# A state-space scan kernel: a small product moved from GpSimd to ScalarE, ScalarE's work reordered, weight loads of the last block spread

## The chip, the cores and the metric

The kernel runs on one NeuronCore of one Trainium2 chip. The metric is the time of one execution on the device, in microseconds. The kernel before took 2678.2 us, the median of three runs (2674.68 to 2682.89).

## The reference, cut to what matters

The input x has the shape (2, 2048, 512). The first half of the model is a small linear recurrence (64 states) followed by a Mamba layer; the second half is a feed-forward layer with quantised activations and weights. What the change touches lies in the Mamba layer:

```python
xb = silu(conv(x_br) + conv_b)                      # 1024 channels
Bm, Cm = xb @ W_b, xb @ W_c                         # 16 states each
delta = softplus(xb @ W_delta + b_delta)
A_bar = exp(delta[..., None] * A)
Bx = delta[..., None] * Bm[:, :, None, :] * xb[..., None]
def step(h, inp):
    a_t, bx_t, c_t = inp
    h = a_t * h + bx_t
    return h, sum(h * c_t[:, None, :], axis=-1)
h0, ys = scan(step, ...)
y = ys + xb * Dp                                    # the product that is moved
out = y * silu(z) @ W_out                           # silu(z) is done at another place
```

The feed-forward half needs its two weights of 4 MB each (`f_w1`, `f_w2`) in SBUF when it starts, and 16 rows of a low-rank factor, made from sixteen 1 MB pieces of `c2_w2` (the chunks).

## The kernel before, in words

The two sequences of 2048 steps are cut into 16 blocks of 256 steps. Within a block the 1024 channels times 16 states are cut into 32 tiles q: channel tile dt = q // 4 (128 channels), state group g = q % 4 (4 states). One tile is a 128x1024 array. Four engines work on each tile:

- ScalarE makes the decay `a_ps` of the tile with four exponentials (L691). There are two such buffers: it may begin tile q when the scan of tile q-2 is over.
- VectorE makes the input term of tile q+1 in a ring of four slots (L845) and then scans tile q (L853).
- GpSimd keeps the last column (L462) and multiplies the scanned states by C in two halves (L469).
- TensorE transposes and sums the result into `yT_ps` (L1056). For each channel tile it first brings in x times D, `xdp` (L1050), which GpSimd makes at g == 0 (L456). VectorE then multiplies by silu(z) into `gbuf` (L788).

Every engine has its own written-out order, and it runs it in order. Between the tiles of block k stand the jobs that prepare block k+1 ("front", `next_plan`), finish the scan's own inputs ("scan", `scan_plan`) and finish block k-1 ("back", `back_plan`). A number in those tables is the tile q before whose exponentials the job stands on ScalarE; TensorE has its own table, with its own numbers. TensorE's jobs go through two PSUM banks, `work0` and `work1`, handed over by the counters `full` and `free`. The jobs of which the prediction speaks:

- DL0 to DL3 are the four parts of `xb @ W_delta` (L1022). TensorE's table has the last quarters of DL1 at 24, of DL2 at 29 and of DL3 at 31. ScalarE takes each with `dexp` (two Abs, L600, two Relu, L602), and each pair of them goes on through `dtail` (Exp, L609) and `dln` (Ln, L613); GpSimd adds the two halves (L420).
- PRJ is the projection of the small recurrence (last part: L932, at 2 in TensorE's table). ScalarE takes it with an Exp (L497) and a Tanh (L500), later an Ln (L505). VectorE's small recurrence, whose first instruction is L746, stands between its scans of tiles 4 and 5 and waits for this Ln.
- `zsilu` is silu(z) (L582). It needs another table of functions, and the exponentials after it need the old one back: an ACT_TABLE_LOAD ahead of it and one behind.

In the last block SyncE's queue carries the chunks and both feed-forward weights. TensorE multiplies the chunks (L1098, two columns) at fixed tiles, the second one at q = 11.

Of the kernel before, what the change touches and what calls it, by code (L numbers as in the profile page):

```python
# [5 lines left out]
ALU = mybir.AluOpType  # L6
ACT = mybir.ActivationFunctionType
# [68 lines left out]
def scan_phase(nc, V, big, s_big, vec, xT_in, w_p, w_s, w_o, w_in, w_bc, w_delta, w_out, f_w1, f_w2, c2_w1, c2_w2,  # L76
# [3 lines left out]
    with ctx:  # L80
# [175 lines left out]
        def _(sp):  # L256
# [11 lines left out]
            def step(k, par, front, back, scan):  # L268
# [19 lines left out]
                if last:

                    sp.wait_ge(full[BANK["WOUT1"]], jobs_before("WOUT1", k) + 1)  # L290
                    sp.dma_start(big[0][:, 0:7 * DI], f_w1[:, 0:7 * DI]).then_inc(s_big[0], 16)
                    sp.dma_start(big[1][:, :], f_w2).then_inc(s_big[1], 16)

                    def keep_row(c):
                        sp.wait_ge(s_rowcp, c + 1)
                        sp.dma_start(lr_dram[c], xw[:, c % 2, :]).then_inc(s_rowst[c % 2], 16)

                    for c in range(1, NCH):
                        if c == 1:
                            sp.wait_ge(full[BANK["WOUT1"]], jobs_before("WOUT1", k) + 1)  # L300
                        if c == 2:
                            sp.wait_ge(s_h, 1)
                        if c >= 3:
                            sp.wait_ge(s_row, c - 2)
                            keep_row(c - 3)
                        sp.dma_start(chunk[(c + 1) % 3], c2_w2[c]).then_inc(s_chunk[c % 3], 16)
                    sp.wait_ge(s_col0, NCOL * NBLK)
                    sp.dma_start(big[0][:, 7 * DI:8 * DI], f_w1[:, 7 * DI:8 * DI]).then_inc(s_big[0], 16)
                    for c in range(NCH - 3, NCH):
                        keep_row(c)  # L310
                    for i in range(2):
                        sp.wait_ge(s_rowst[i], 16 * NCH // 2)
# [39 lines left out]
        def _(pool):  # L352
# [69 lines left out]
            def step(k, par, front, back, scan):  # L422
                for q in range(NQ):
# [25 lines left out]
                            r.then_inc(s_cpow, 1)  # L449
                    if not scan:  # L450
                        continue
                    if g == 0:

                        wait(pool, s_xb, 2 * k + (2 if dt >= ND // 2 else 1))
                        wait(pool, s_tr, NQ * k + NG * (dt - 2) + 1)
                        nc.gpsimd.tensor_tensor(xdp[:, dt % 2, :], xb[:, par, dt, :],  # L456
                                                V[:, V_DP + dt:V_DP + dt + 1].to_broadcast([P, T]), ALU.mult)\
                            .then_inc(s_xdp, 1)

                    pool.wait_ge(s_scan, NQ * k + q + 1)  # L460
                    h = ring[:, q % RING, :, :]
                    nc.gpsimd.tensor_tensor(carry[:, par, dt, G * g:G * g + G].rearrange("p (g o) -> p g o", o=1),  # L462
# [12 lines left out]
        def _(act):  # L475
# [9 lines left out]
            def step(k, par, front, back, scan):  # L485
# [6 lines left out]
                def prj():  # L492

                    ps = take("PRJ")
                    if isinstance(k, int) and k == -1:
                        act.wait_ge(s_setD, 8)
                    nc.scalar.activation(e0[:, :], ps[0:N0, 0:T], ACT.Exp, bias=sc0[0:N0, 4:5]).then_inc(s_e0, 1)  # L497

                    wait(act, s_c0, 6 * n)
                    nc.scalar.activation(c0[:, :], ps[N0:P, 0:T], ACT.Tanh, bias=sc0[N0:P, 4:5]).then_inc(s_tanh, 1)  # L500

                def prj_ln():
                    nc.scalar.preload_act_table_set("natural_log_exp_and_others")
                    act.wait_ge(s_c0, 6 * n + 1)
                    nc.scalar.activation(e0[:, :], e0[:, :], ACT.Ln, bias=1.0).then_inc(s_l0, 1)  # L505

# [69 lines left out]
                def zsilu():  # L576

                    for j in (2, 3):
                        act.wait_ge(free[BANK[f"Z{j}"]], jobs_before(f"Z{j}", k) + 1)
                    for tt in range(NT):  # L580
                        v = zs[:, fp, tt, :]
                        r = nc.scalar.activation(v, v, ACT.Silu)  # L582
                    r.then_inc(s_zs, 1)

# [35 lines left out]
                def gT(pair, gp):  # L620
# [3 lines left out]
                                         ps[:, :].rearrange("p (m t) -> p m t", m=2), ACT.Copy)\  # L624
                        .then_inc(free[BANK[f"GT{pair}"]], 1)

                def gelu():
                    act.wait_ge(s_h, 1)
                    for m in range(KD):
                        r = nc.scalar.activation(hT[:, m, :], work[0][:, 8 + 2 * m:8 + 2 * m + 2], ACT.Gelu,  # L630
                                                 bias=V[:, V_C2B1 + m:V_C2B1 + m + 1])
                    r.then_inc(s_hT, 1)

                def rowcopy(c):
# [4 lines left out]
                    else:  # L639
# [1 line left out]
                    nc.scalar.activation(xw[:, c % 2, :], work[0][0:2, :], ACT.Copy).then_inc(s_rowcp, 1)  # L641


                next_plan = {5: [prj], 6: [prj_ln], 8: [lambda: stats(0)], 9: [lambda: stats(1)], 10: [y0scale],
                             11: [y0back], 14: [lambda: xcopy(0)], 15: [lambda: xcopy(1)], 16: [lambda: xcopy(2)],
                             17: [lambda: xcopy(3), silu], 20: [bc], 21: [lambda: zcopy(0)], 23: [lambda: zcopy(1)],
                             25: [lambda: dexp(0, False)], 27: [lambda: zcopy(2), lambda: dexp(1, False), lambda: dtail(0, False)],
                             28: [lambda: zcopy(3), lambda: dln(0, False)], 30: [zsilu],
                             31: [lambda: dexp(2, False)]}
                scan_plan = {2: [lambda: dexp(3, True), lambda: dtail(1, True)], 6: [lambda: dln(1, True)]}  # L650
                turned = {13: 0, 20: 1, 28: 2}
                back_plan = {6: [lambda: gT(ND // 2 - 1, fp)], 9: [lambda: wout(0)], 12: [lambda: wout(1)]}
                for q in range(NQ + 1):
# [496 lines left out]
def ffn_phase(nc, V, big, s_big, x_in, x2_dram, lr_dram, c2_b2, base, b1, b2, out):  # L1150

    ctx = ExitStack()
    with ctx:
# [21 lines left out]
        with setup:  # L1175
# [39 lines left out]
            def _(act):  # L1215

                for i, q in enumerate((q1, q2)):
                    act.wait_ge(s_big[i], 32 if i == 0 else 16)
                    nc.scalar.activation(q[:, :, :].rearrange("p a b -> p (a b)"), big[i][:, :], ACT.Abs,
                                         accum_out=mq[:, i:i + 1]).then_inc(z["abs"], 1)  # L1220

# [439 lines left out]
```

## Time and profile before

| | |
|---|---|
| median of three runs | 2678.2 us (2674.68 to 2682.89) |
| profiled execution, its own time | 2683.99 us |
| span of the profiled execution | 2681.9 us |
| mean granted clock of TensorE | 0.948 |
| busy, share of the span | TensorE 86%, weight loads 59%, VectorE 84%, ScalarE 62%, GpSimd 64% |
| first and last scan (L853) start | 118.9 and 2157.2 us |

Busy times of different engines lie beside each other and don't add up. The part from the first scan to the last is three quarters of the span. In the lists of waits a row names the instruction that waited, then what released it. The chain of waits that the page prints lies for the most part in the feed-forward half, so it says little about the blocks; there the timeline has to be read.

### The profile page before, as it was taken

The numbers are of one execution on the slowest core, as the hardware profiler recorded it, in microseconds if no ns is written. First come the engines' busy times: TensorE is split into PE (matmuls) and PEld (weight loads), VectorE is DVE, ScalarE is ACT, GpSimd is POOL, SyncE is SP. The second block draws the span as 40 slices with busy tenths as digits, with TensorE's granted clock in tenths as the row PEclk, the third lists the DMA queues.
The fourth block names the chain that finished last, engine by engine and source line by source line (L and its number), as shares of the span: only waits on it lengthen the run. The fifth ranks groups of instructions, "written<-read, shape, count | busy, mean of one in ns | idle before, by whom it ended". The sixth has DMA issues, their size and how long they took to land. (4 is left out here: it accounts for less than half of the span.)

```text
span 2681.9 us, 34173 instructions
## 1 busy us (share of the span) xinstructions
PE 2307.7 (86%) x11488; PEld 1590.2 (59%) x11520; DVE 2265.7 (84%) x2232; ACT 1665.4 (62%) x3332; POOL 1725.8 (64%) x2042
## 2 busy tenths in 40 slices
PE   7878888889898988888988888898986884999997
PEld 5656666666666665766666666666664332444443
DVE  2299999999999999999999999999997735888886
ACT  2566676666667676667676767667674434555554
POOL 0287777878787877878787878787876521232221
PEclk8889999999999999999999999999997987999999
DMA  4102020202011110202020202010114421112110
GB/s 184 72 1 71 9 74 7 75 11 74 17 63 45 36 64 17 72 10 71 9 71 9 75 5 79 17 63 25 48 57 178 175 100 55 60 59 66 63 52 24
DMA packets 47435, 151.74 MB, mean 57 GB/s; under 512 B 7973, under 2 KB 8869, under 8 KB 44206
## 3 DMA queue, kind: packets, MB, share of 16 engines
q1 hardware_dynamic: 47278, 149.76, 15.8%
q8 instruction: 84, 1.38, 0.2%
q14 instruction: 73, 0.60, 0.1%
HBM read 132.37 MB, written 17.37 MB: 56 GB/s over the span
## 5 line engine op out<-in xcount | busy, mean ns | idle before, releaser
L469 POOL TENSOR_TENSOR ring<-ring,Cbc 128x512 f32<-128x512 f32 x1024 | 1281.8, 1273 | 44.6 <-POOL carry L462 0.4
L853 DVE TENSOR_TENSOR_SCAN ring<-a_ps,ring 128x1024 f32<-128x1024 f32 x512 | 1168.0, 2282 | 99.3 <-ACT a_ps L691 97.9
L691 ACT ACTIVATE a_ps<-delta,nA 128x255 f32<-128x255 f32 x2048 | 850.0, 466 | 382.2 <-DVE ring L853 381.0
L1056 PE MATMUL yT_ps<-ident,ring 128*128 128x128 f32 x4096 | 586.0, 284 | 171.2 <-POOL ring L469 168.7
L845 DVE TENSOR_TENSOR ring<-u_ps,Bbc 128x1024 f32<-128x1024 f32 x512 | 619.7, 1210 | 38.1 <-PE yT_ps L1056 31.3
L1056 PEld LDWEIGHTS yT_ps<-ident,ring 128*128 128x128 f32 x4096 | 474.1, 144 | 287.9 <-POOL ring L469 245.6
L1022 PE MATMUL work<-xb,big 128*128 128x256 f32 x2048 | 474.5, 383 | 11.1 <-ACT zs L557 11.1
L1022 PEld LDWEIGHTS work<-xb,big 128*128 128x128 f32 x2048 | 384.4, 192 | 80.1 <-issue 17.8
L462 POOL TENSOR_TENSOR carry<-ring,half 128x4 f32<-128x4 f32 x512 | 126.0, 246 | 380.4 <-DVE ring L853 378.8
L1038 PE MATMUL work<-Wout,xb 128*128 128x512 f32 x512 | 242.1, 608 | 0.0
L995 PE MATMUL work<-y0s,big 128*128 128x256 f32 x1024 | 235.1, 380 | 0.7 <-issue 0.7
L1396 POOL TENSOR_TENSOR m<-m,pows 128x1 f32<-128x1 f32 x64 | 34.1, 548 | 311.0 <-DVE m L1528 311.0
L995 PEld LDWEIGHTS work<-y0s,big 128*128 128x128 f32 x1024 | 188.8, 190 | 24.7 <-issue 1.0
L1038 PEld LDWEIGHTS work<-Wout,xb 128*128 128x128 f32 x512 | 100.4, 201 | 120.4 <-issue 120.4
L1463 PE MATMUL o_ps<-q,qhT 128*128 128x512 bf16 x481 | 112.1, 386 | 18.9 <-DVE qhT L1561 18.7
L420 POOL TENSOR_TENSOR delta<-delta,lnbuf 128x1024 f32<-128x1024 f32 x32 | 75.5, 2361 | 74.4 <-ACT lnbuf L613 74.4
L1427 PE MATMUL x_ps<-lay,x2T 128*128 128x512 f32 x256 | 121.9, 621 | 0.7 <-ACT x2T L1488 0.7
L564 ACT ACTIVATE xb<-work,V 128x256 f32<-128x256 f32 x128 | 53.3, 467 | 103.9 <-PE work L995 103.9
L1442 PE MATMUL h_ps<-q,qaT 128*128 128x512 bf16 x511 | 115.5, 379 | 0.1
L1494 ACT ACTIVATE hb<-hb 128x2048 f32<-128x2048 f32 x32 | 61.1, 1911 | 65.8 <-DVE hb L1547 65.8
L824 DVE TENSOR_TENSOR u_ps<-delta,xb 128x510 f32<-128x510 f32 x64 | 58.5, 914 | 48.0 <-POOL delta L420 48.0
L1011 PE MATMUL work<-xb,Wbc 128*32 128x256 f32 x256 | 70.2, 437 | 33.2 <-ACT xb L573 33.2
(198 smaller groups left out, 2538.9 us busy)
## 6 DMA issues: line engine op xcount, KB each, us to landing
Bbc<-bc_rows SPq DMA_DIRECT2D x64, 512.0 KB, 4.6
Cbc<-bc_rows SPq DMA_DIRECT2D x64, 512.0 KB, 3.7
xT<-in_xT SPq DMA_DIRECT2D x16, 514.0 KB, 3.6
x_rows<-x2row SPq DMA_DIRECT2D x32, 256.0 KB, 2.0
xp<-x_rows SPq DMA_DIRECT2D x32, 256.0 KB, 2.7
xx<-in_x SPq DMA_DIRECT2D x32, 256.0 KB, 3.0
out_rows<-orow SPq DMA_DIRECT2D x32, 256.0 KB, 2.0
delta<-in_c_w SPq DMA_DIRECT2D x6, 1024.0 KB, 5.1
```

The lines of the kernel that those rows point to most:

```text
L462: nc.gpsimd.tensor_tensor(carry[:, par, dt, G * g:G * g + G].rearrange("p (g o) -> p g o", o=1), h[:, :, T - 1:T], ident1, ALU.mult).then_ ...
L469: nc.gpsimd.tensor_tensor(hp, hp, Cbc[:, G * g + GP * c:G * g + GP * c + GP, :], ALU.mult)\
L691: r = nc.scalar.activation(a_ps[q % 2][:, i, 1:T], delta[:, par, dt, 1:T], ACT.Exp, scale=nA[:, dt, s:s + 1])
L845: dve.tensor_tensor(ring[:, q % RING, :, :], u_ps[:, dt % 2:dt % 2 + 1, :].to_broadcast([P, G, T]), Bbc[:, G * g:G * g + G, :], ALU.mult). ...
L853: dve.tensor_tensor_scan(ring[:, q % RING, :, :].rearrange("p g t -> p (g t)"), a_ps[q % 2][:, :, :].rearrange("p g t -> p (g t)"), ring[: ...
L995: r = pe.matmul(ps[:, T * m:T * m + T], Mx[:, tap, c:c + P], y0s[:, fp, tap:tap + T], start=(tap == 0), stop=(tap == 3))
L1022: r = pe.matmul(ps[:, T * m:T * m + T], Wd[:, d, c:c + P], xb[:, fp, d, :], start=(d == 0), stop=(d == ND - 1))
L1038: r = pe.matmul(ps[:, :], xb[:, fp, d, P * tt:P * tt + P], Wout[:, d, :], start=False, stop=(d == ND - 1))
L1056: r = pe.matmul(yT_ps[:, tt, :], ring[:, q % RING, i, P * tt:P * tt + P], ident[:, :], is_transpose=True, start=False, stop=(g == NG - 1 a ...
L1427: r = pe.matmul(x3_ps[:, :], x2T[:, d, :], lay[:, batch, d, :], start=(d == 0), stop=(d == KD - 1))
L1442: r = pe.matmul(h_ps[:, 512 * c:512 * c + 512], qaT[:, d, :], q1[:, d, 512 * c:512 * c + 512], start=(d == 0), stop=(d == KD - 1))
L1463: r = pe.matmul(o_ps[:, :], qhT[:, d, :], q2[:, d, :], start=(d == 0), stop=(d == KF - 1))
```

## The change

Three parts:

1. `xdp` is made by ScalarE (`skip`, an ACT.Copy with D as its scale), at the last tile of the channel tile before: at q = 3, 7, ... 27 for dt+1, and at q = 29 for the first channel tile of the next block. GpSimd has none of it left.
2. ScalarE's jobs stand at other tiles. The Exp of PRJ goes from 5 to 3. silu(z) goes from 30 of the block before to 4 of the block that uses it, the Tanh goes with it to 4, one table load ahead of both and one behind. `dexp(0)` goes from 25 to 24, `dexp(1)` from 27 to 26, `dln(0)` from 28 to 27, `dexp(3)` from 2 to 1. The table load ahead of the Ln at 6 is gone.
3. In the last block `f_w2` is loaded early, behind the first chunk, and `f_w1` in eight pieces, one behind each of the chunks 2 to 8 and the last as before. Before, both were issued ahead of chunk 1.

```diff
                     sp.dma_start(chunk[1], c2_w2[0]).then_inc(s_chunk[0], 16)
+                    sp.wait_ge(full[BANK["DL3"]], jobs_before("DL3", k - 1) + 1)
+                    sp.dma_start(big[1][:, :], f_w2).then_inc(s_big[1], 16)
...
-                    sp.wait_ge(full[BANK["WOUT1"]], jobs_before("WOUT1", k) + 1)
-                    sp.dma_start(big[0][:, 0:7 * DI], f_w1[:, 0:7 * DI]).then_inc(s_big[0], 16)
-                    sp.dma_start(big[1][:, :], f_w2).then_inc(s_big[1], 16)
...
                         sp.dma_start(chunk[(c + 1) % 3], c2_w2[c]).then_inc(s_chunk[c % 3], 16)
+                        if 2 <= c < 9:
+                            sp.dma_start(big[0][:, DI * (c - 2):DI * (c - 1)], f_w1[:, DI * (c - 2):DI * (c - 1)])\
+                                .then_inc(s_big[0], 16)
...
-                    if g == 0:
-                        wait(pool, s_xb, 2 * k + (2 if dt >= ND // 2 else 1))
-                        wait(pool, s_tr, NQ * k + NG * (dt - 2) + 1)
-                        nc.gpsimd.tensor_tensor(xdp[:, dt % 2, :], xb[:, par, dt, :],
-                                                V[:, V_DP + dt:V_DP + dt + 1].to_broadcast([P, T]), ALU.mult)\
-                            .then_inc(s_xdp, 1)
...
+                def skip(b, bp, dt):
+                    wait(act, s_xb, 2 * b + (2 if dt >= ND // 2 else 1))
+                    wait(act, s_tr, NQ * b + NG * (dt - 2) + 1)
+                    nc.scalar.activation(xdp[:, dt % 2, :], xb[:, bp, dt, :], ACT.Copy, scale=V[:, V_DP + dt:V_DP + dt + 1])\
+                        .then_inc(s_xdp, 1)
...
+                    if q == 4 and (front or scan):
+                        nc.scalar.preload_act_table_set("silu_and_others")
+                        if scan:
+                            zsilu()
+                        if front:
+                            prj_tanh()
+                        nc.scalar.preload_act_table_set("natural_log_exp_and_others")
...
+                    if scan and g == 3 and dt < ND - 1:
+                        skip(k, par, dt + 1)
+                    if front and q == NQ - 3:
+                        skip(n, fp, 0)
```

ScalarE, first tiles of a block, the kernel before, from the exponentials of tile 2 (the L691 row ahead of L497 holds tiles 2, 3 and 4):

```order
L600 ACTIVATE lnbuf<-work,V 128x256
L602 ACTIVATE delta<-work,V 128x256
L609 ACTIVATE lnbuf<-lnbuf 128x1024
L691 ACTIVATE a_ps<-delta,nA 128x255 x12
L497 ACTIVATE e<-work,sc 64x256
L500 ACTIVATE c<-work,sc 64x256
L691 ACTIVATE a_ps<-delta,nA 128x255 x4
L623 ACTIVATE xb<-work 128x512
L503 ACT_TABLE_LOAD
L505 ACTIVATE e<-e 64x256
L613 ACTIVATE lnbuf<-lnbuf 128x1024
L691 ACTIVATE a_ps<-delta,nA 128x255 x8
```

The same place in the changed kernel, from tile 1 on (L707 are the exponentials, L628 is `xdp`, L492 and L498 the Exp and Tanh of PRJ, L579 is silu(z)):

```order
L707 ACTIVATE a_ps<-delta,nA 128x255 x4
L606 ACTIVATE lnbuf<-lnbuf 128x1024
L707 ACTIVATE a_ps<-delta,nA 128x255 x4
L492 ACTIVATE e<-work,sc 64x256
L628 ACTIVATE xdp<-xb,V 128x256
L707 ACTIVATE a_ps<-delta,nA 128x255 x4
L674 ACT_TABLE_LOAD
L579 ACTIVATE zs<-zs 128x1024 x2
L498 ACTIVATE c<-work,sc 64x256
L679 ACT_TABLE_LOAD
L707 ACTIVATE a_ps<-delta,nA 128x255 x8
L620 ACTIVATE xb<-work 128x512
```

The Exp of PRJ and `xdp` now stand ahead of the exponentials of tile 3, and two table loads with silu(z) and the Tanh between them ahead of those of tile 4.

ScalarE, tiles 25 to 29 of a block, before (L557 copies z):

```order
L691 ACTIVATE a_ps<-delta,nA 128x255 x8
L557 ACTIVATE zs<-work 128x512
L600 ACTIVATE lnbuf<-work,V 128x256
L602 ACTIVATE delta<-work,V 128x256
L600 ACTIVATE lnbuf<-work,V 128x256
L602 ACTIVATE delta<-work,V 128x256
L609 ACTIVATE lnbuf<-lnbuf 128x1024
L691 ACTIVATE a_ps<-delta,nA 128x255 x4
L557 ACTIVATE zs<-work 128x512
L613 ACTIVATE lnbuf<-lnbuf 128x1024
L623 ACTIVATE xb<-work 128x512
L691 ACTIVATE a_ps<-delta,nA 128x255 x8
```

And now, from tile 24 on (L597 and L599 are `dexp`, L554 copies z, L606 and L610 are `dtail` and `dln`):

```order
L707 ACTIVATE a_ps<-delta,nA 128x255 x8
L597 ACTIVATE lnbuf<-work,V 128x256
L599 ACTIVATE delta<-work,V 128x256
L597 ACTIVATE lnbuf<-work,V 128x256
L599 ACTIVATE delta<-work,V 128x256
L707 ACTIVATE a_ps<-delta,nA 128x255 x4
L554 ACTIVATE zs<-work 128x512
L606 ACTIVATE lnbuf<-lnbuf 128x1024
L610 ACTIVATE lnbuf<-lnbuf 128x1024
L628 ACTIVATE xdp<-xb,V 128x256
L707 ACTIVATE a_ps<-delta,nA 128x255 x4
L554 ACTIVATE zs<-work 128x512
```

`dexp(1)` now stands ahead of the exponentials of tile 26; before, it stood ahead of those of tile 27, behind the copy of z.

SyncE's queue in the last block, before (L279 and L281 are the first two loads for the factor rows, L286 stores results, L291 and L292 are the two weights, L306 the chunks, L296 stores a row of the factor):

```order
L279 DMA delta<-in_c_w 128x2048
L281 DMA zs<-in_c_w 128x2048
L286 DMA x_rows<-x2row 128x512 x2
L291 DMA big<-in_f_w 128x7168
L292 DMA big<-in_f_w 128x8192
L306 DMA xb<-in_c_w 128x2048
L306 DMA delta<-in_c_w 128x2048
```

And now:

```order
L281 DMA zs<-in_c_w 128x2048
L284 DMA big<-in_f_w 128x8192
L289 DMA x_rows<-x2row 128x512 x2
L305 DMA xb<-in_c_w 128x2048
L305 DMA delta<-in_c_w 128x2048
L308 DMA big<-in_f_w 128x1024
L295 DMA lr_rows<-lnbuf 2x512
```

`f_w2` stands ahead of the stores of results, and chunk 1 directly behind them.

## Rows read from the trace of the kernel before

**Rows 1.** Waits of the whole span: who, released by, us in total, times, longest

```profile
DVE ring L853 <- ACT a_ps L691: 97.9, 62, 4.0
DVE ring L845 <- PE yT_ps L1056: 31.3, 17, 22.6
```

**Rows 2.** Timeline, VectorE, tiles 23, 26, 27, 31 (start, duration, [idle before])

```profile
964.87 2.28 DVE L853 TENSOR_TENSOR_SCAN ring<-a_ps,ring 128x1024 f32<-128x1024 f32 x1
...
975.13 2.28 DVE L853 TENSOR_TENSOR_SCAN ring<-a_ps,ring 128x1024 f32<-128x1024 f32 x1
...
979.66 2.29 DVE L853 TENSOR_TENSOR_SCAN ring<-a_ps,ring 128x1024 f32<-128x1024 f32 x1 [0.91 <-ACT a_ps L691]
...
994.22 2.29 DVE L853 TENSOR_TENSOR_SCAN ring<-a_ps,ring 128x1024 f32<-128x1024 f32 x1 [0.89 <-ACT a_ps L691]
```

**Rows 3.** Timeline, TensorE, the same stretch: transpose of tile 23, DL1, DL2

```profile
970.07 0.66 PE L1056 MATMUL yT_ps<-ident,ring 128*128 128x128 f32 x4 [0.56 <-POOL ring L469]
970.56 3.62 PE L1022 MATMUL work<-xb,big 128*128 128x256 f32 x16
...
985.35 7.07 PE L1022 MATMUL work<-xb,big 128*128 128x256 f32 x32
```

**Rows 4.** Timeline, ScalarE, the same stretch

```profile
975.07 0.60 ACT L557 ACTIVATE zs<-work 128x512 f32<-128x512 f32 x1 [2.91 <-PE work L1003]
...
976.99 1.08 ACT L609 ACTIVATE lnbuf<-lnbuf 128x1024 f32<-128x1024 f32 x1
977.94 1.69 ACT L691 ACTIVATE a_ps<-delta,nA 128x255 f32<-128x255 f32 x4
...
984.73 1.28 ACT L582 ACT_TABLE_LOAD   x1
986.02 2.00 ACT L582 ACTIVATE zs<-zs 128x1024 f32<-128x1024 f32 x2
```

**Rows 5.** Timeline, start of the next block, several engines: DL3, PRJ, tiles 0, 4 and L746

```profile
999.61 0.47 ACT L600 ACTIVATE lnbuf<-work,V 128x256 f32<-128x256 f32 x1 [1.40 <-PE work L1022]
...
1000.89 2.28 DVE L853 TENSOR_TENSOR_SCAN ring<-a_ps,ring 128x1024 f32<-128x1024 f32 x1
...
1001.05 1.07 ACT L609 ACTIVATE lnbuf<-lnbuf 128x1024 f32<-128x1024 f32 x1
...
1006.73 1.95 PE L932 MATMUL work<-xT,Ws 128*64 128x256 f32 x8
...
1015.27 2.27 DVE L853 TENSOR_TENSOR_SCAN ring<-a_ps,ring 128x1024 f32<-128x1024 f32 x1
...
1018.12 0.47 DVE L746 SCALAR_TENSOR_TENSOR e<-work,sc,e 64x256 f32<-64x256 f32 x1 [0.58 <-ACT e L505]
```

**Rows 6.** Groups by line of the whole span: count, busy us, mean ns

```profile
L456 POOL TENSOR_TENSOR xdp<-xb,V 128x256 f32<-128x256 f32 x128 | 78.9, 617 | 0.1
...
L602 ACT ACTIVATE delta<-work,V 128x256 f32<-128x256 f32 x128 | 60.4, 472 | 0.0
```

**Rows 7.** Timeline, last block, TensorE: chunks 1 and 2

```profile
2079.59 6.07 PE L1098 MATMUL work<-xb,Wtap 128*2 128x512 f32 x8 [18.45 <-DMA xb<-in_c_w]
...
2087.49 3.59 PE L1098 MATMUL work<-delta,Wtap 128*2 128x512 f32 x8
```

**Rows 8.** Timeline, last block, SyncE's DMA issues

```profile
2056.11 0.43 SPq L291 DMA_DIRECT2D big<-in_f_w  x1
...
2057.08 0.43 SPq L306 DMA_DIRECT2D xb<-in_c_w  x1
```

**Rows 9.** The page's DMA issues: KB each, median us from issue to landing

```profile
delta<-in_c_w SPq DMA_DIRECT2D x6, 1024.0 KB, 5.1
```

**Rows 10.** Timeline, VectorE and GpSimd at two changes of block

```profile
745.20 0.67 DVE L824 TENSOR_TENSOR u_ps<-delta,xb 128x510 f32<-128x510 f32 x1
...
995.13 2.50 POOL L469 TENSOR_TENSOR ring<-ring,Cbc 128x512 f32<-128x512 f32 x2
996.42 1.77 DVE L824 TENSOR_TENSOR u_ps<-delta,xb 128x510 f32<-128x510 f32 x1
```

More of the change, by code:

```diff
@@ L497, in prj, with prj_tanh @@
                     nc.scalar.activation(e0[:, :], ps[0:N0, 0:T], ACT.Exp, bias=sc0[0:N0, 4:5]).then_inc(s_e0, 1)
+                def prj_tanh():
+                    ps = take("PRJ")
                     wait(act, s_c0, 6 * n)
@@ L502, in prj_ln @@
                 def prj_ln():
-                    nc.scalar.preload_act_table_set("natural_log_exp_and_others")
                     act.wait_ge(s_c0, 6 * n + 1)
@@ L578, in zsilu @@
                     for j in (2, 3):
-                        act.wait_ge(free[BANK[f"Z{j}"]], jobs_before(f"Z{j}", k) + 1)
+                        act.wait_ge(free[BANK[f"Z{j}"]], jobs_before(f"Z{j}", k - 1) + 1)
                     for tt in range(NT):
-                        v = zs[:, fp, tt, :]
+                        v = zs[:, par, tt, :]
                         r = nc.scalar.activation(v, v, ACT.Silu)
@@ L641, in rowcopy @@
                     nc.scalar.activation(xw[:, c % 2, :], work[0][0:2, :], ACT.Copy).then_inc(s_rowcp, 1)
-                next_plan = {5: [prj], 6: [prj_ln], 8: [lambda: stats(0)], 9: [lambda: stats(1)], 10: [y0scale],
+                next_plan = {3: [prj], 6: [prj_ln], 8: [lambda: stats(0)], 9: [lambda: stats(1)], 10: [y0scale],
                              11: [y0back], 14: [lambda: xcopy(0)], 15: [lambda: xcopy(1)], 16: [lambda: xcopy(2)],
                              17: [lambda: xcopy(3), silu], 20: [bc], 21: [lambda: zcopy(0)], 23: [lambda: zcopy(1)],
[L647 to L650, printed above, removed]
+                             24: [lambda: dexp(0, False)], 26: [lambda: dexp(1, False)],
+                             27: [lambda: zcopy(2), lambda: dtail(0, False), lambda: dln(0, False)],
+                             28: [lambda: zcopy(3)], 31: [lambda: dexp(2, False)]}
+                scan_plan = {1: [lambda: dexp(3, True)], 2: [lambda: dtail(1, True)], 6: [lambda: dln(1, True)]}
                 turned = {13: 0, 20: 1, 28: 2}
@@ L1217, in _ @@
                 for i, q in enumerate((q1, q2)):
-                    act.wait_ge(s_big[i], 32 if i == 0 else 16)
+                    act.wait_ge(s_big[i], 16 * (F * KD // DI) if i == 0 else 16)
                     nc.scalar.activation(q[:, :, :].rearrange("p a b -> p (a b)"), big[i][:, :], ACT.Abs,
```

## The prediction, made before the changed kernel was run

> **What bounds the kernel now.** I read three views, in this order.
>
> The list of waits first. VectorE is busy 84% of the span, and in the blocks it is the engine that the others wait for. What holds VectorE itself up is the first row: its scans wait 97.9 us for ScalarE's exponentials, in 62 places, and its input terms wait 31.3 us for TensorE, of which 22.6 us is one single wait [rows 1].
>
> Then VectorE's timeline of one block, to see at which tiles those waits lie. The 97.9 us are some 6 us in each of 16 blocks; 0.91 us stands ahead of tile 27 and 0.89 ahead of tile 31 [rows 2], and the largest one stands behind the first silu of a block (tile 17), whose place the change leaves alone. Since nothing else stops the scans of a block, each us by which ScalarE comes late for a tile is a us of the block, and each us freed on an engine that waits is nothing.
>
> Then ScalarE and TensorE beside it, for the question that decides here: at the place where a job stands now, is its input there, and how much room is there before the scan?
>
> **GpSimd's product.** GpSimd loses 128 products of 617 ns, 78.9 us in all [rows 6]. It is no gain by itself: GpSimd waits for VectorE's scans. ScalarE gets the 128. The trace has no Copy of this shape from SBUF; the nearest row is a Relu of 128x256 with a mean of 472 ns [rows 6], and four instructions of that kind go from 999.61 to 1001.05, 0.36 us a piece, because each overlaps the one before [rows 5]. I take 0.36 (0.3 to 0.47). At most tiles ScalarE idles before its exponentials and covers it; where it is already late, at tiles 3 and 27, the 0.36 is in the sums below. Its buffer and its inputs are ready several tiles ahead.
>
> **The end of a block (tiles 26 to 31).** `dexp(1)` moves one tile forward, but its input does not. TensorE first transposes tile 23, for which it waits for GpSimd and so for the scan of tile 23 (start 964.87), and then runs the 16 instructions of DL1's last half, from 970.56 for 3.62 us: DL1 is full at 974.18, 9.31 us after the start of scan 23 [rows 2, 3]. Before, ScalarE took it behind the copy of z at 975.07, where it had waited 2.91 us with the exponentials of tile 26 already done [rows 4]. Now these exponentials stand behind it. 974.18 + 0.04 + 1.44 (`dexp`) + 1.67 (four exponentials) + 0.03 = 977.36, where scan 26 started at 975.13 [rows 2, 4, 5]: 2.2 us late. None of the 9.31 us is work that the change takes away.
>
> Tile 27: the exponentials of 26 leave the engine's entrance at 977.26; the copy of z takes 0.50, `dtail` 0.95 (976.99 to 977.94), `dln` as much and 0.13 for waiting on its end, `xdp` 0.36: 980.14, and the exponentials end at 981.85 where scan 27 stood at 979.66 [rows 2, 4]. Still 2.2 late; the 0.91 that was idle is used up in it.
>
> Tiles 28 to 30 have room, and at 30 silu(z) is gone: table load 1.28, 2.00 for two functions, and one load more [rows 4]. But tile 31 stands behind `dexp(2)`, which needs DL2. TensorE began this stretch at 985.35, 5.69 after scan 27, and DL2 is full after 24 of the 32 instructions, 5.3 us on [rows 2, 3]. With scan 27 at 981.86 this gives 992.85, and + 0.04 + 1.44 + 1.67 + 0.03 = 996.03, where scan 31 started at 994.22. So the block ends **1.8 us later**. The gain of moving silu(z) away is at most the waits at 30 and 31, and most of it is lost again in DL2. Bounds: below, the 0.9 us that the waits of 27 and 31 could give back if DL1 came early (-2.6 with tile 30); above, 2.2.
>
> **The start of a block (tiles 1 to 5).** `dexp(3)` at 1: it started at 999.61, waiting for TensorE [rows 5]. Behind it now come the exponentials of tile 1, done by 1002.8, while scan 0 (1000.89 to 1003.17) still runs: covered.
>
> The Exp of PRJ at 3: PRJ is full at 1006.73 + 1.95 = 1008.68, 7.79 after scan 0 [rows 5]. The exponentials of tile 3 now stand behind this Exp. One after the other from 1008.72: Exp 0.45, `xdp` 0.36, exponentials of tile 3 1.67, load 1.28, two silu 2.00, Tanh 0.43, load 1.28, exponentials of tile 4 1.67, and 0.03 to the scan: 1017.9, where scan 4 started at 1015.27 [rows 4, 5, 6]: 2.6 us late. Part of it comes back at once. VectorE's small recurrence (L746) waited 0.58 us for the Ln behind a table load that is gone. Now ScalarE does the exponentials of tile 5 (1.6), the copy of GT3 (0.6) and the Ln (0.42) from 1017.8: 1020.4, against 1018.12 [rows 5]. The start costs **2.3 us**. Bounds: 0 if PRJ came 2.3 us earlier, 2.4 with the dearer `xdp`.
>
> [...]
>
> **Sum over blocks.** Fifteen blocks of 16 have a next one to prepare: 15 x (1.8 + 2.3) = 61.5 us. In the first block there is no work of a block before, and DL3 is late there; I leave 3 us either way. In the last block neither the Exp nor the Tanh is there, and silu with two loads (4.56) fits ahead of tile 4; silu(z) in the run-up before block 0 stood in a wait for TensorE.
>
> **The last block.** The 22.6 us wait is this: the feed-forward weights were issued at 2056.11, chunk 1 behind them at 2057.08 [rows 8], and TensorE waited 18.45 us for it; the product then took 6.07 instead of the 3.59 of the next one [rows 7]. Now chunk 1 goes out about 2056.1, a lone chunk lands in 5.1 us [rows 9], so at 2061.2, and TensorE is there at 2079.59 - 18.45 = 2061.14. The pieces of 512 KB go behind chunks that are waited for only later, and `f_w2` runs when nothing else is under way. Gain 18.45 + 2.48 = **20.9 us** (15, if the pieces delay a chunk; 22.6 at most, the whole wait).
>
> **Total.** 2683.99 (the profiled execution's own time) + 61.5 - 20.9 = 2724.6 us. That execution lay 5.8 over the median of the runs, so for the median: 2678.2 + 40.6 = **2719 us**. The case's own range is 2706 to 2731: 15 blocks by +-0.6 us, the last block and the first by some us.
>
> **Rivals.**
>
> *The reordering is covered* (faster). Place: tiles 26 and 4. It decides from the point at which DL1 and PRJ are full 2.2 us and 2.6 us earlier against the scans. For it: GpSimd, which TensorE waits for, has less to do. Against it: TensorE waits at 970.07 for tile 23's product with C, and GpSimd makes that as soon as the scan is over, with `xdp` elsewhere [rows 3]. Then the block waits fall by 2.6 in 15 blocks and the last block gives 20.9: 2678.2 - 39 - 20.9 = 2618; with only the stalls gone, 2657. Chance 0.07.
>
> *Only one of the two delays is there* (no change, or little). If PRJ were early and tile 26 late: 2678.2 + 15 x 1.8 - 20.9 = 2684; the other way round 2692. Nothing in the rows speaks for it. Chance 0.06, half of it within the bound.
>
> *VectorE gets past GpSimd at the change of block* (slower, but less). L824 took 1.77 us at 996.42, while a GpSimd instruction ran, and 0.67 us at 745.20 [rows 10]. GpSimd's place in time at the end of a block shifts with the change, by less than one of its 1.25 us instructions by my reckoning. If VectorE comes first in 14 blocks: 2719 - 15.4 = 2704. [...] Chance 0.12.
>
> *The last block's wait moves instead of going* (slower still). If a chunk behind the pieces is late by what is now gone: 2678.2 + 61.5 = 2740. Against it: seven pieces of 512 KB over seven rows of the factor, each behind its chunk in the queue, and a lone chunk needs 5.1 us. Chance 0.07.
>
> **How the numbers follow.** Forecast 0.68, rivals 0.07, 0.06, 0.12, 0.07. The range of 8 in 10 is 2692 to 2733: it takes in the forecast's own range and the rival with the lock, and leaves the faster one and most of the last out. A change within 0.3% (8 us) is what a measurement of this kernel can't tell from none. Faster by more: 0.07. Within: 0.04. Slower by more: 0.89.
>
> **What would show it.** Right: scans of tile 26 wait some 2.2 us and of tile 4 some 2.6 us for ScalarE's exponentials, in 15 blocks; the time from one block's first scan to the next grows by about 4; VectorE's total wait for exponentials rises from 97.9 to over 150 us; the row of 22.6 is gone and TensorE's wait for chunk 1 is under 1 us. Wrong: the Abs of DL1 starts without idle time ahead of it at tile 26, or the second chunk still waits.

## The result, and the profile after

The changed kernel takes 2726.7 us (median of 4 runs, 2726.1 to 2737.9), the kernel before 2678.0 in the same series (2674.7 to 2682.9). The ratio is 1.019, with a 95% interval of 1.016 to 1.0221: some 49 us slower. The forecast was 2719 us, in a range of 2692 to 2733. The execution that was profiled is the longest of the four (2737.85 us, span 2736.1); the spans of the other three lie at 2723 to 2725.

The list of waits first (who, released by: us in total, times, longest), of the kernel after:

```profile
DVE ring L869 <- ACT a_ps L707: 175.6, 77, 6.4
...
DVE ring L861 <- PE yT_ps L1072: 17.8, 22, 2.9
```

L869 is the scan and L861 the input term. The scans wait for the exponentials 175.6 us instead of 97.9, and the wait of 22.6 us for the last block's weights is gone, the longest of its kind being 2.9 now [rows 1]. One grew by 78 us, the other shrank by 13.5.

VectorE's timeline of one block with its change to the next, for comparison with [rows 2, 5]; the rows are the scans of tiles 23, 26, 27 and 31, the first term of the next block (L840), its scans 0 and 4, and the small recurrence (L762):

```profile
997.99 2.28 DVE L869 TENSOR_TENSOR_SCAN ring<-a_ps,ring 128x1024 f32<-128x1024 f32 x1
...
1010.49 2.29 DVE L869 TENSOR_TENSOR_SCAN ring<-a_ps,ring 128x1024 f32<-128x1024 f32 x1 [2.15 <-ACT a_ps L707]
...
1015.00 2.29 DVE L869 TENSOR_TENSOR_SCAN ring<-a_ps,ring 128x1024 f32<-128x1024 f32 x1 [0.89 <-ACT a_ps L707]
...
1029.33 2.29 DVE L869 TENSOR_TENSOR_SCAN ring<-a_ps,ring 128x1024 f32<-128x1024 f32 x1 [1.77 <-ACT a_ps L707]
1031.54 1.42 DVE L840 TENSOR_TENSOR u_ps<-delta,xb 128x510 f32<-128x510 f32 x1
...
1035.65 2.28 DVE L869 TENSOR_TENSOR_SCAN ring<-a_ps,ring 128x1024 f32<-128x1024 f32 x1
...
1052.76 2.29 DVE L869 TENSOR_TENSOR_SCAN ring<-a_ps,ring 128x1024 f32<-128x1024 f32 x1 [2.64 <-ACT a_ps L707]
1055.28 0.47 DVE L762 SCALAR_TENSOR_TENSOR e<-work,sc,e 64x256 f32<-64x256 f32 x1 [0.23 <-ACT e L502]
...
1165.89 2.28 DVE L869 TENSOR_TENSOR_SCAN ring<-a_ps,ring 128x1024 f32<-128x1024 f32 x1
...
1297.26 2.28 DVE L869 TENSOR_TENSOR_SCAN ring<-a_ps,ring 128x1024 f32<-128x1024 f32 x1
```

From scan 23 to scan 26 it is 12.50 us here and was 10.26, to scan 27 17.01 and was 14.79, to scan 31 31.34 and was 29.35. From scan 0 to scan 4 it is 17.11 and was 14.38. This block goes from scan 0 at 1035.65 to the next one's at 1165.89, 130.24 us. Before, the fifteen blocks ahead of the last took 126.1 on average, and 126.15 in the steady ones. The next block here takes 131.37, more than the forecast has; that comes below.

ScalarE in the same stretch: `dexp(1)`, the exponentials of tile 26, and in the next block the Exp of PRJ, the silu group and the exponentials of tiles 4 and 5:

```profile
1007.33 0.47 ACT L597 ACTIVATE lnbuf<-work,V 128x256 f32<-128x256 f32 x1 [5.36 <-PE work L1038]
...
1008.78 1.68 ACT L707 ACTIVATE a_ps<-delta,nA 128x255 f32<-128x255 f32 x4
...
1043.49 0.47 ACT L492 ACTIVATE e<-work,sc 64x256 f32<-64x256 f32 x1 [2.78 <-PE work L948]
1043.86 0.50 ACT L628 ACTIVATE xdp<-xb,V 128x256 f32<-128x256 f32 x1
1044.26 1.66 ACT L707 ACTIVATE a_ps<-delta,nA 128x255 f32<-128x255 f32 x4
1045.94 1.28 ACT L674 ACT_TABLE_LOAD   x1
1047.23 2.01 ACT L579 ACTIVATE zs<-zs 128x1024 f32<-128x1024 f32 x2
...
1049.76 1.28 ACT L679 ACT_TABLE_LOAD   x1
1051.05 3.27 ACT L707 ACTIVATE a_ps<-delta,nA 128x255 f32<-128x255 f32 x8
```

ScalarE stands idle 5.36 us ahead of `dexp(1)`, with tile 26's exponentials behind it in the program and their input ready. Ahead of the Exp of PRJ it stands idle 2.78 us, with tile 3's behind it. And TensorE's side of both, DL1's last half, DL2 and PRJ:

```profile
1003.67 3.62 PE L1038 MATMUL work<-xb,big 128*128 128x256 f32 x16
...
1020.79 7.07 PE L1038 MATMUL work<-xb,big 128*128 128x256 f32 x32
...
1041.51 1.94 PE L948 MATMUL work<-xT,Ws 128*64 128x256 f32 x8
```

DL1 is full at 1003.67 + 3.62 = 1007.29, 9.30 us after scan 23 (9.31 before). PRJ is full 7.80 us after scan 0 (7.79 before), and DL2 starts 5.79 us after scan 27 (5.69 before). TensorE keeps its distance to the scans, so a job of ScalarE that is put one tile forward still starts only when TensorE is through, and what stands behind the job waits with it.

In the last block, TensorE's product of chunk 1:

```profile
2134.60 3.59 PE L1114 MATMUL work<-xb,Wtap 128*2 128x512 f32 x8 [1.25 <-ACT lnbuf L645]
```

It waits 1.25 us, here for ScalarE and no longer for the DMA, where it had waited 18.45, and takes 3.59 instead of 6.07 us [rows 7]. From scan 12 to scan 13 of the last block it is 6.63 us and was 26.31.

### The profile page after: what moved, and what is told of

Same layout as the page of the kernel before. It is cut to its first block and busy times, and to the rows that moved or that the text cites. A ratio compares the mean times of both kernels' runs of the same rounds, so it can differ in the third digit from the quotient of the medians.

```text
span 2736.1 us, 34209 instructions
## 1 busy us (share of the span) xinstructions
PE 2338.7 (85%) x11520; PEld 1608.2 (59%) x11520; DVE 2261.6 (83%) x2232; ACT 1692.6 (62%) x3443; POOL 1657.4 (61%) x1914
## 5 line engine op out<-in xcount | busy, mean ns | idle before, releaser
L869 DVE TENSOR_TENSOR_SCAN ring<-a_ps,ring 128x1024 f32<-128x1024 f32 x512 | 1168.3, 2282 | 175.6 <-ACT a_ps L707 175.6
L707 ACT ACTIVATE a_ps<-delta,nA 128x255 f32<-128x255 f32 x2048 | 852.0, 468 | 221.5 <-DVE ring L869 220.6
L1072 PEld LDWEIGHTS yT_ps<-ident,ring 128*128 128x128 f32 x4096 | 482.5, 146 | 272.8 <-POOL ring L464 229.7
L861 DVE TENSOR_TENSOR ring<-u_ps,Bbc 128x1024 f32<-128x1024 f32 x512 | 620.1, 1211 | 24.5 <-PE yT_ps L1072 17.8
L1038 PE MATMUL work<-xb,big 128*128 128x256 f32 x2048 | 482.7, 388 | 39.1 <-ACT zs L554 39.1
L1054 PE MATMUL work<-Wout,xb 128*128 128x512 f32 x512 | 252.3, 629 | 0.0
L597 ACT ACTIVATE lnbuf<-work,V 128x256 f32<-128x256 f32 x128 | 60.9, 476 | 235.4 <-PE work L1038 235.4
L1054 PEld LDWEIGHTS work<-Wout,xb 128*128 128x128 f32 x512 | 102.9, 206 | 125.3 <-issue 125.3
L1479 PE MATMUL o_ps<-q,qhT 128*128 128x512 bf16 x512 | 119.2, 387 | 11.4 <-DVE qhT L1577 11.4
```

The source lines that it names most:

```text
L707: r = nc.scalar.activation(a_ps[q % 2][:, i, 1:T], delta[:, par, dt, 1:T], ACT.Exp, scale=nA[:, dt, s:s + 1])
L861: dve.tensor_tensor(ring[:, q % RING, :, :], u_ps[:, dt % 2:dt % 2 + 1, :].to_broadcast([P, G, T]), Bbc[:, G * g:G * g + G, :], ALU.mult). ...
L869: dve.tensor_tensor_scan(ring[:, q % RING, :, :].rearrange("p g t -> p (g t)"), a_ps[q % 2][:, :, :].rearrange("p g t -> p (g t)"), ring[: ...
L1038: r = pe.matmul(ps[:, T * m:T * m + T], Wd[:, d, c:c + P], xb[:, fp, d, :], start=(d == 0), stop=(d == ND - 1))
L1054: r = pe.matmul(ps[:, :], xb[:, fp, d, P * tt:P * tt + P], Wout[:, d, :], start=False, stop=(d == ND - 1))
L1072: r = pe.matmul(yT_ps[:, tt, :], ring[:, q % RING, i, P * tt:P * tt + P], ident[:, :], is_transpose=True, start=False, stop=(g == NG - 1 a ...
```

## The experiments

All times are medians; the interval is that of the ratio to the kernel before, in runs beside it.

**Only the loads spread** (the kernel before, with the last block's weight loads as in the kernel after):

```
+ sp.wait_ge(full[BANK["DL3"]], ...)                   # behind DL3 of the block before:
+ sp.dma_start(big[1][:, :], f_w2)
...
+ if 2 <= c < 9:                                      # behind chunk c
+     sp.dma_start(big[0][:, DI*(c-2):DI*(c-1)], f_w1[:, DI*(c-2):DI*(c-1)])
- sp.dma_start(big[0][:, 0:7*DI], f_w1[:, 0:7*DI])      # ahead of chunk 1
- sp.dma_start(big[1][:, :], f_w2)
```

> The kernel before with only the loads of the last block spread; all else as before. Theory (the wait for chunk 1 is a queue effect and goes): 2678 - 20.9 = 2657 us, VectorE's 22.6 us wait falls to about 2, the step from scan 12 to 13 of the last block from 26.3 to under 7. Rival (the wait moves to a later chunk): 2678, and a wait of TensorE for a DMA of over 10 us at another chunk.

Measured: 2660.5 us (2653.5 to 2665.6), ratio 0.9933 (0.9914 to 0.9953). The last block takes 124.4 us instead of 149.35, the others 126.1 on average as before. The product of the second chunk, for which TensorE had waited 18.45 us, now waits 1.24 us for it:

```profile
2053.48 3.59 PE L1101 MATMUL work<-xb,Wtap 128*2 128x512 f32 x8 [1.24 <-DMA xb<-in_c_w]
```

So this part is a gain by itself, and its mechanism is the forecast's: 18.45 - 1.24 of waiting and 2.48 of duration are 19.7 us, and from scan 12 to scan 13 it is 6.63 instead of 26.31 us, 19.7 as well. The medians differ by 18 us. The last block of the two traces differs by 25, of which the other 5.3 us are waits of VectorE for TensorE at tiles 9, 11 and 19 that are missing or shorter in this execution. The granted clock in the last block was 0.68 from 2040 to 2050 in the kernel before and 1.00 from 2025 on in this one, and the kernel after, with the same loads, has these waits again; so the 5.3 us belong to the execution and not to the loads. The profiled execution is also the fastest of its four, and its first scan starts at 113.7 us instead of 118.9, though nothing ahead of it was changed.

**Only the product on ScalarE** (the kernel before, with `skip` in place of GpSimd's product):

```
- nc.gpsimd.tensor_tensor(xdp[:, dt % 2, :], xb[:, par, dt, :], V[:, V_DP+dt:...], ALU.mult)
+ nc.scalar.activation(xdp[:, dt % 2, :], xb[:, bp, dt, :], ACT.Copy, scale=V[:, V_DP+dt:...])
```

> The kernel before with only the product of x and D moved to ScalarE. Theory (GpSimd's relief is worth nothing, ScalarE covers the product): 2676 to 2684 us, tile 27 later by 0.36 us, at the change of block L824 still blocked. Rival (GpSimd's relief lets VectorE past it and brings TensorE forward): 2660 or less, L824 at 0.67 us. Second rival (ScalarE is full and pays for each product): 2678 + 128 x 0.36 = 2724.

Measured: 2683.95 us, ratio 1.0014 (1.0004 to 1.0025). The row of the product by line (count, busy us, mean ns of one):

```profile
L623 ACT ACTIVATE xdp<-xb,V 128x256 f32<-128x256 f32 x128 | 64.5, 504 | 0.0
```

By its list of waits the scans wait 111.2 us for the exponentials, 13.3 us more than before, but the whole is only 5.5 us longer by the medians (1 to 7 by the interval). The product's duration is 504 ns, while two that follow each other start some 0.4 us apart: in the kernel after the Copy starts at 1043.86 and the exponentials at 1044.26.

The whole grows so little because two effects run against each other. By the starts of the scans, the steps up to tiles 27 and 30, where ScalarE is late, are 0.4 us longer each, 11.9 us in fifteen blocks; the step up to tile 9, where VectorE waits for TensorE, takes 3.6 us more in all (whether the product or a longer fall of TensorE's clock makes the latter isn't shown). Against that the change of block is 0.9 us shorter, 13.5 us in all, since VectorE's first term of a block now hardly meets GpSimd:

```profile
996.96 1.27 POOL L461 TENSOR_TENSOR ring<-ring,Cbc 128x512 f32<-128x512 f32 x1
...
997.98 0.80 DVE L827 TENSOR_TENSOR u_ps<-delta,xb 128x510 f32<-128x510 f32 x1
```

It takes 0.77 to 0.86 us at the fifteen changes of block, where it took 1.77 at fourteen of them [rows 10]. GpSimd's instruction starts 1.02 us ahead of it, and started 0.06 us ahead before. So the time fell just inside the expected range by a cancellation that the expectation did not have: it said that this term would still be blocked. The relief of GpSimd is worth 13.5 us at the change of block, by the rival's mechanism, and what the product costs elsewhere is slightly more.

**DL1's jobs back** (the kernel after, with the jobs of DL1 where they stood in the kernel before):

```
- 26: [dexp(1)], 27: [zcopy(2), dtail(0), dln(0)], 28: [zcopy(3)]
+ 27: [zcopy(2), dexp(1), dtail(0)], 28: [zcopy(3), dln(0)]
```

> The changed kernel with the two Abs, two Relu and Exp of DL1 back behind the copy of z at tile 27 and the Ln at 28. Theory (tile 26 waits for DL1 because of where dexp(1) stands): no wait at 26, 0.9 to 1.3 us at 27, the block 1.8 us shorter than in the changed kernel, about 2727 - 27 = 2700 us. Rival (the end of the block is late because ScalarE has the extra products): 2720 or more, the waits at 26 to 31 keep their sum.

Measured: 2707.2 us (2704.5 to 2710.8), ratio 1.0105 (1.0085 to 1.0125): 19.6 us less than the kernel after. Its scans of tiles 26, 27 and 31:

```profile
994.30 2.28 DVE L869 TENSOR_TENSOR_SCAN ring<-a_ps,ring 128x1024 f32<-128x1024 f32 x1
999.23 2.29 DVE L869 TENSOR_TENSOR_SCAN ring<-a_ps,ring 128x1024 f32<-128x1024 f32 x1 [1.32 <-ACT a_ps L707]
...
1013.46 2.29 DVE L869 TENSOR_TENSOR_SCAN ring<-a_ps,ring 128x1024 f32<-128x1024 f32 x1 [1.49 <-ACT a_ps L707]
```

The wait at 26 is gone, so `dexp(1)` at 26 made it. The kernel ends 7 us above the expectation: most of its blocks take 129.5 to 129.7, not 128.4, since at tiles 8 and 9 VectorE waits 1.4 to 1.7 us for TensorE (0.35 in the steady blocks before), the place at which some blocks of the kernel after are long, too.

**The silu group a tile later** (the kernel after, with the Exp of PRJ at 4 and the group at 5, ahead of tile 5's exponentials):

```
- next_plan = {3: [prj], 6: [prj_ln], ...        back_plan = {6: [gT(3)], ...
+ next_plan = {4: [prj], ...                     back_plan = {5: [gT(3)], ...
- if q == 4 and (front or scan):   # load, silu(z), tanh, load
+ if q == 5 and (front or scan):   # the same, and prj_ln() behind it
```

> The changed kernel with the two table loads, silu(z) and Tanh ahead of the exponentials of tile 5 instead of 4, the Exp of PRJ at 4 instead of 3, the copy of GT3 and the Ln of PRJ at 5. Theory (tile 5 has VectorE's small recurrence ahead of its scan, so 5 us of ScalarE fit there): no wait at tile 4, L746 about where it was before, the block 2.3 to 2.6 us shorter, and TensorE's clock does not fall at the start of blocks, together 2680 to 2692 us. Rival (silu(z) with two loads costs the same at any tile, as ScalarE has 5 us more at a stretch than its two buffers hold): 2720 or more, the wait moves to tile 5.

Measured: 2693.0 us (2692.1 to 2694.2), ratio 1.0048 (1.0031 to 1.0065): 33.7 us less than the kernel after, and 1 us above the expected range. Scans 0 and 4 and the small recurrence:

```profile
1141.15 2.28 DVE L871 TENSOR_TENSOR_SCAN ring<-a_ps,ring 128x1024 f32<-128x1024 f32 x1
...
1155.53 2.27 DVE L871 TENSOR_TENSOR_SCAN ring<-a_ps,ring 128x1024 f32<-128x1024 f32 x1
1158.62 0.48 DVE L764 SCALAR_TENSOR_TENSOR e<-work,sc,e 64x256 f32<-64x256 f32 x1 [0.82 <-ACT e L502]
```

From scan 0 to 4 it is 14.38 us again, as before, and the steady blocks take 128.1 (two of them 128.4). Tiles 26 and 31 still wait as in the kernel after, so the two delays are separate. No block is stretched at tiles 8 and 9: in the two traces fifteen blocks are 38.5 us shorter in all, more than 15 x 2.1. That TensorE's clock would not fall at the start of a block did not come true: it falls there in every block still (0.57 from 255 to 260, 0.75 in the next 5 us), for a shorter time.

**The jobs of DL1 and DL2 late** (the last kernel, with more of ScalarE's jobs moved):

```
- 26: [dexp(1)], 27: [zcopy(2), dtail(0), dln(0)], 28: [zcopy(3)], 31: [dexp(2)]
+ 27: [zcopy(2), dexp(1)], 28: [zcopy(3), dtail(0)], 29: [dln(0)], 32: [dexp(2)]
- scan_plan = {1: [dexp(3)], 2: [dtail(1)], 6: [dln(1)]}
+ scan_plan = {2: [dexp(3), dtail(1)], 6: [dln(1)]}
```

> The kernel after, with four groups of ScalarE's jobs put elsewhere: the silus and the tanh ahead of tile 5's exponentials (as in the run before), the two exponentials of delta that stood at tiles 26 and 30 moved to tile 27 and behind tile 31's last exponentials, the fourth one to tile 2 of the next block. Theory (each row of exps that comes late adds its time to VectorE's end): the waits of VectorE at tiles 26, 27 and 31, 4.7 us a block in the run before, go, the block takes 123.4 to 123.6 us instead of 128.1, and the kernel about 2621 us, faster than the kernel before as well. Rival (the exponential behind tile 31 delays the next block's first scans or TensorE's projection): a new wait of 1 to 3 us at tiles 0 to 2 takes the place, and the kernel stays above 2655 us.

Measured: 2632.0 us (2631.4 to 2635.2), ratio 0.9826 (0.9806 to 0.9846). The scans' wait for ScalarE is 61.3 us in all; at 26 and 31 there is none, and at 27 some 0.4 in most blocks. The kernel lies 11 us above the expectation, since the steady blocks take 124.3 to 124.7 us, not 123.5: a wait of 1.26 us is new ahead of the input term of tile 1, where the rival put one. Its mechanism is another, though. TensorE there, and VectorE's row that waits:

```profile
847.09 7.07 PE L1041 MATMUL work<-xb,big 128*128 128x256 f32 x32
854.00 0.38 PE L1069 MATMUL yT_ps<-ident,xdp 128*128 128x128 f32 x2
854.22 1.04 PE L1075 MATMUL yT_ps<-ident,ring 128*128 128x128 f32 x8
855.10 3.62 PE L1041 MATMUL work<-xb,big 128*128 128x256 f32 x16
858.55 1.04 PE L1075 MATMUL yT_ps<-ident,ring 128*128 128x128 f32 x8
```

```profile
859.62 0.16 DVE L855 TENSOR_REDUCE Bbc<-big 128x4 f32<-128x4 f32 x1 [1.26 <-PE yT_ps L1075]
```

TensorE has no idle time from 847.09 to the transposes at 858.55: it doesn't wait for the late exponentials, but is simply full, with 48 instructions of DL2 and DL3 ahead of what VectorE wants. With ScalarE's waits gone, TensorE is next. Whether another order of these products would help was not tried.

**The silu of x in two halves** (the last kernel, tile 17):

```
- 17: [xcopy(3), silu]           # load, silu of both halves, load
+ 17: [silu(0), xcopy(3), silu(1)]
```

> The kernel v1 with the silu at tile 17 cut into two halves: the first stands where ScalarE waits for the PSUM bank of the last copy of x (1.9 us), the second behind that copy, so that less work stands between tile 17's exponentials and the scan that wants them. Theory: VectorE's wait at tile 17, 3.6 us a block in all kernels so far, falls to about 1.7 us, the block by 2.0 us, the kernel by some 30 us against v1 (about 2591 us if v1 takes 2621). Rival (the wait at tile 17 is set by TensorE and not by ScalarE): no change against v1.

Measured: 2603.3 us (2602.3 to 2604.1), ratio 0.9714 (0.9695 to 0.9733). ScalarE at tile 17:

```profile
906.09 1.28 ACT L567 ACT_TABLE_LOAD   x1
907.38 1.06 ACT L572 ACTIVATE xb<-xb 128x1024 f32<-128x1024 f32 x1
908.35 0.82 ACT L561 ACTIVATE xb<-work,V 128x256 f32<-128x256 f32 x2
909.26 1.06 ACT L572 ACTIVATE xb<-xb 128x1024 f32<-128x1024 f32 x1
910.34 1.28 ACT L574 ACT_TABLE_LOAD   x1
```

The load and the first half fill the time in which ScalarE had waited 1.93 us for the product of the last x. VectorE's wait at tile 17 falls from 3.7 to 1.8 us, the block to 122.45. So at least half of the largest wait of a block, there in all kernels, was ScalarE's order and not TensorE.

**The product back on GpSimd** (the last kernel, with the multiplication where it stood in the kernel before).

> The kernel v2 with the product of x and D on GpSimd again, where it stood in the kernel before; ScalarE's order and the spread weight loads stay. Theory (the product's engine matters only where ScalarE is late, 0.36 to 0.4 us in one or two places of a block): within 8 us of v2, and rather below it. Rival (the relief of GpSimd is worth something once ScalarE's order is mended): more than 8 us slower than v2.

Measured: 2597.8 us (2594.0 to 2598.6), ratio 0.9691 (0.967 to 0.9711): 5.4 us less than the kernel with it on ScalarE. The size is that of the product's move alone, but the account differs: nearly all of it (6.0 us in fifteen blocks) stands in the step up to tile 27, and at the change of block VectorE's first term is short in both (0.67 us with the product on ScalarE, mostly 0.82 here). This is the fastest version, 3.1% below the kernel before. The spread loads, the later silu(z) with one table load less, and `dexp(0)` at 24 stem from the change; its other moves do not.

## Why the prediction was right

**The end of a block.** Forecast: scans of tiles 26, 27 and 31 later by 2.2, 2.2 and 1.8 us. Measured in the block above: 2.24, 2.22 and 1.99. `dexp(1)` starts 9.34 us after scan 23, 0.04 after DL1 is full, as the forecast has it. The experiment that puts these jobs back removes the wait at 26.

**The start of a block.** Forecast: scan 4 later by 2.6 us, of which 0.35 comes back at the small recurrence, 2.3 in all. Measured: 17.11 against 14.38, 2.73, with a wait of 0.23 instead of 0.58 at the recurrence, so 2.4. Moving the group by one tile gives back 2.1 us in each steady block (130.2 to 128.1), and the two ends are independent, as assumed: the waits at 26 and 31 stay.

**Their sum.** 4.1 us a block in the forecast, and 126.15 to 130.24 in five of the fourteen blocks behind the first. But four take 130.5 to 130.6 and five 131.3 to 131.8, so that with the first block fifteen came to 71.3 us more in the profiled execution, not 61.5. **This is the term that was too small.** In the fourteen blocks the excess over 4.1 us each is 7.7 us in all, and most of it (6.4) stands in a stretch that the forecast left unchanged, tiles 8 and 9. The scan of tile 4 and two waits in the block that starts at 251, and windows of it (busy us per engine, then the granted clock of TensorE as a share of full speed):

```profile
268.24 2.29 DVE L869 TENSOR_TENSOR_SCAN ring<-a_ps,ring 128x1024 f32<-128x1024 f32 x1 [2.64 <-ACT a_ps L707]
...
285.02 1.23 DVE L861 TENSOR_TENSOR ring<-u_ps,Bbc 128x1024 f32<-128x1024 f32 x1 [0.54 <-PE yT_ps L1072]
...
289.28 1.23 DVE L861 TENSOR_TENSOR ring<-u_ps,Bbc 128x1024 f32<-128x1024 f32 x1 [0.84 <-PE yT_ps L1072]
```

```profile
255.00:265.00 10.00, 7.86 (x42) 5.11 (x40) 9.93 (x10) 7.16 (x13) 7.24 (x10) 0.88 0.17 53
265.00:270.00 5.00, 2.23 (x8) 1.43 (x8) 2.36 (x2) 4.94 (x11) 2.21 (x2) 0.50 0.00 0
270.00:275.00 5.00, 4.47 (x6) 1.92 (x7) 4.62 (x10) 3.67 (x8) 4.31 (x4) 0.50 0.01 3
275.00:280.00 5.00, 5.00 (x16) 2.46 (x15) 5.00 (x3) 2.28 (x6) 3.39 (x4) 0.88 0.00 0
```

While VectorE waits at tile 4, TensorE has little to do (2.23 of 5 us busy), and its granted clock is at 0.50 from 265 to 275, the lower of the two levels in this trace (1.00 and 0.50 of full speed). The fall begins before the stall: the stall starts at 265.60 (268.24 - 2.64), and the mean of 0.88 up to 265 means some 2.4 us at 0.50 by then. TensorE then runs the products behind the stall at nearly half the pace (1.06 us each for `wout`'s at L1054 instead of 0.59) and is late for VectorE. In the block that takes 130.24 the clock also falls, but less of it meets these products:

```profile
1050.00:1055.00 5.00, 1.84 (x8) 1.14 (x8) 2.36 (x2) 4.96 (x11) 1.72 (x2) 0.60 0.00 0
1055.00:1060.00 5.00, 4.96 (x9) 2.24 (x10) 4.62 (x10) 3.19 (x7) 4.79 (x4) 0.72 0.00 0
```

Counted over the trace, the blocks sort themselves by it: two products of 1.06 us behind the stall in each of the five blocks of 130.2 us, three in the four of 130.6, five in the five of 131.3 to 131.8. In the experiment with DL1's jobs back it is the same, 3 in the block of 128.5 and 5 or 6 in those of 129.4 to 130.0. So the blocks with a stall at tile 4 pay more than its length, 0.3 to 1.6 us in nine of fourteen. The kernel before, without the stall, has a fall at this place too (0.52 from 258.9 to 265.6), and VectorE waits only 0.35 to 0.64 us at tile 9 there. Where the stall is gone (the group at 5) slow products still occur, up to four, but VectorE's wait at tile 9 stays at 0.45 us, and the block takes 128.1 with one and with four. That the lower clock stretches the block, and that the stall makes the fall longer, is read from these counts; no run changed the clock alone, and what makes one block's fall longer than the next's is open.

**The first block.** I left 3 us either way. It took 131.5 instead of 125.3, 6.2 more, which is 2.1 over the 4.1 of the others: within the margin, and on its dear side. `dexp(3)` at tile 1 is late there, as feared; the wait:

```profile
126.57 2.29 DVE L869 TENSOR_TENSOR_SCAN ring<-a_ps,ring 128x1024 f32<-128x1024 f32 x1 [3.30 <-ACT a_ps L707]
```

In the kernel with `dexp(3)` back at tile 2 the first block waits 0.74 us in its place.

**The last block.** Forecast 20.9 us less, measured 19.6 in the profiled execution (149.35 to 129.77), by the mechanism forecast; what is missing is a wait of 1.25 us that is left at chunk 1, where the forecast named under 1 us as the sign. The same last block took 124.1 us in the experiment with DL1's jobs back, and there TensorE's clock stayed up, as it did in the experiment on the loads. The rows are windows of 10 us, from 20 us after its first scan on, first of the kernel after, then of that experiment:

```profile
2102.00:2112.00 10.00, 10.00 (x37) 5.33 (x36) 9.89 (x12) 3.95 (x9) 9.24 (x10) 0.98 0.04 17
2112.00:2122.00 10.00, 10.00 (x54) 8.68 (x53) 7.11 (x6) 6.34 (x15) 6.13 (x9) 0.70 0.03 10
```

```profile
2077.00:2087.00 10.00, 10.00 (x38) 5.42 (x37) 9.89 (x11) 3.93 (x9) 9.71 (x10) 1.00 0.07 26
2087.00:2097.00 10.00, 10.00 (x60) 7.36 (x59) 10.00 (x8) 5.86 (x15) 6.60 (x11) 1.00 0.01 2
```

**The rivals.** The covered reordering and the single delay are out: both waits are there. VectorE does not get past GpSimd at the change of block, but comes later in its instruction: L840 takes 1.42 us in the block above and up to 1.58 in others (1.77 and 0.67 before [rows 10]), and the step from scan 31 to the next scan 0 is 3.2 us shorter in fifteen blocks, 0.2 each, not 1.1. With the product's move alone it gains nearly the whole, 0.9. The longer VectorE's instruction took, the more of GpSimd's was left at its start: 1.77 us with 1.21 left in the kernel before, 1.42 with 0.86 left in the kernel after, 0.80 with 0.25 left with the product's move alone. VectorE's ends 0.56 us behind GpSimd's in the kernel before (998.19 and 997.63, [rows 10]), 0.56 in the kernel after (1032.96 and 1032.40) and 0.55 with the product's move alone (998.78 and 998.23). This is the rival that the forecast's range calls the one with the lock; the runs show these times and no lock. The last block's wait did not move. The product's 0.36 us was right in size: 0.4 us between starts, and 0.4 us more at each tile where ScalarE is late. The 5.5 us for the kernel are that cost less the gain at the change of block. So the forecast's sentence that GpSimd's relief is no gain by itself is wrong at that place: with the product moved alone it is worth 13.5 us. The sum has nothing for it, and the forecast has it as a rival; in the kernel after 3.2 us are left of it.

**Against the median.** Forecast +40.8, measured +48.7 us. The profiled execution alone shows +54: 71.3 in the blocks, 19.6 back in the last one, 2.5 ahead of and behind them. It is 11 us above the other three, whose mean granted clock was 0.939 and not 0.933, and they have no trace; how much of the excess in the blocks is in the median as well is open.

One reading was off without harm: the 97.9 us of waits are not in each of 16 blocks. Fifteen blocks have 6.2 us each at tiles 17, 27, 30 and 31, the last one has none, and 4.7 us stand at the first tiles of the first block, with the longest wait of all (4.0) ahead of the very first scan.

## What to carry to other kernels

When a job on an in-order engine is moved forward, look at when its input is ready against the work that will now stand behind it: if the engine already idled ahead of the job, the move buys nothing, and each us up to the input is a us of whoever waits for the work behind (2.24 us at scan 26 here). Fill such idle time with work that has its input, and put jobs with a late consumer behind the work that has an early one; here that took 29 us (a silu cut in two) and 61 us (four groups of ScalarE's jobs) off. After that, read again who is late: it was TensorE, which no row of the kernel before names at that place. And before work is moved to relieve an engine, look where that engine's instructions meet those of the one that decides: in the order of the kernel before, GpSimd's relief was worth 13.5 us at the change of block, and the same product's cost on ScalarE hid it.

## What the runs showed of the hardware that had not been expected

Around a stall of 2.6 us on VectorE, TensorE's granted clock was at its lower level for more than 10 us (0.50 from 265 to 275, 0.88 in the windows beside them), and of fourteen blocks with the same instructions nine were 0.3 to 1.6 us longer, in a stretch four tiles behind the stall.

In the last block the granted clock fell to a mean of 0.70 in a stretch in which TensorE was busy 10.00 of 10 us and had been for 10 us before (2112 to 2122). It fell to 0.68 at the same place in the kernel before (2040 to 2050, busy 10.00 of 10). The kernel with the same code there as the kernel after kept 1.00, and the block differed by 5.6 us. What decided between the two is open.

Each load of ScalarE's tables took 1.28 us in all nine traces, and next to nothing was lost around the one at the start of a block in the kernel after: the exponentials ahead of it end at 1045.92, it starts at 1045.94, and the silu starts at 1047.23, 0.01 us behind it. There are four loads a block in the kernel after and those made from it, and five in the kernel before.

VectorE's first term of a block (128x510, from `delta` and `xb`) took 0.67 us at one change of block of the kernel before and 1.77 at another (745.20 and 996.42), for the same work. Where it started during an instruction of GpSimd's, in the three changes of block above, it took what was left of that one (1.21, 0.86 and 0.25 us) and 0.55 or 0.56 us more.
